# Maxima of the scores by four heads instead of two, and new instruction orders, in the first two of four passes of a decoder kernel

## What is computed

```python
x = _layernorm(x + _L0_attn_ref(x, Wq, Wk, Wv))              # self attention, 16 heads of 16
x = _layernorm(x + _L0_xattn_ref(x, ctx, ctx, ...))          # cross attention over 77 keys
x = _layernorm(x + _L0_ffn_ref(x, w_gate, w_up, w_down))     # quantized gated MLP
x = _layernorm(x + _L1_attn_ref(x, ...))                     # self attention with rotary embedding
x = _layernorm(x + _L1_xattn_ref(ctx, x))                    # alignment by dynamic time warping
x = _layernorm(x + _L1_ffn_ref(x, ...))                      # attention with gated heads
```

## Time and profile before

| | |
|---|---|
| median of 3 runs | 5856.48 us (5843.52 to 5859.08) |
| the profiled execution | 5858.39 us |
| its span in the profile | 5856.6 us |
| PE busy | 5289.1 us (90%) |
| DVE busy | 4889.5 us (83%) |
| ACT busy | 4166.3 us (71%) |
| POOL busy | 2753.9 us (47%) |

### The profile page before, as it was taken

How to read it: one execution, slowest core, us unless ns; L and a number is a source line. 1 busy time by engine, 2 the same in 40 slices (tenths; PEclk the granted TensorE clock), 3 DMA queues, 4 the chain that set the end, 5 groups by cost and what they waited for, 6 DMA issues and landing times. The chain is left out here.

```text
span 5856.6 us, 138862 instructions
## 1 busy us (share of the span) xinstructions
PE 5289.1 (90%) x54914; PEld 3660.6 (63%) x54914; DVE 4889.5 (83%) x11487; ACT 4166.3 (71%) x7921; POOL 2753.9 (47%) x2766
## 2 busy tenths in 40 slices
PE   6999999969999999987999999999308999999998
PEld 4666666646666666655666666666206667666666
DVE  6888888859999999986878778778677888888887
ACT  5777777748888888875666666666326777777776
POOL 0122111125555555543545545545106777777775
PEclk9999999989999999999999999999659999999999
DMA  1111111111111111001010010010110001101000
GB/s 55 45 45 45 48 45 46 45 36 30 30 30 30 31 30 29 30 23 35 30 34 30 30 34 30 30 34 30 38 30 14 31 26 31 31 26 31 28 29 23
DMA packets 140516, 194.01 MB, mean 33 GB/s; under 512 B 26080, under 2 KB 63840, under 8 KB 139488
## 3 DMA queue, kind: packets, MB, share of 16 engines
q1 hardware_dynamic: 139872, 185.13, 10.1%
HBM read 112.90 MB, written 72.18 MB: 32 GB/s over the span
## 5 line engine op out<-in xcount | busy, mean ns | idle before, releaser
L1020 ACT ACTIVATE Cpr<-pj 128x512 f32<-128x512 f32 x1024 | 522.2, 614 | 426.9 <-PE pj L814 426.9
L1206 DVE TENSOR_REDUCE Amp<-pj 128x2 f32<-128x512 f32 x1024 | 629.5, 682 | 97.8 <-PE pj L881 97.8
L1206 DVE TENSOR_REDUCE Cmp<-pj 128x2 f32<-128x512 f32 x1024 | 634.4, 682 | 77.7 <-PE pj L881 77.7
L1020 ACT ACTIVATE Apr<-pj 128x512 f32<-128x512 f32 x1024 | 522.1, 613 | 172.7 <-PE pj L814 172.7
L1206 DVE TENSOR_REDUCE Dmp<-pj 128x2 f32<-128x512 f32 x1024 | 633.2, 681 | 6.1 <-PE pj L881 6.1
L1020 ACT ACTIVATE Dpr<-pj 128x512 f32<-128x512 f32 x1024 | 520.2, 610 | 101.1 <-PE pj L814 101.0
L1134 POOL TENSOR_SCALAR Ave<-Amv 128x2 f32<-128x2 f32 x64 | 14.6, 228 | 971.7 <-DVE Amv L1274 971.7
L1106 POOL TENSOR_TENSOR Dnrm<-Dnrm,power 128x32 f32<-128x32 f32 x64 | 348.8, 5449 | 122.7 <-DVE Dnrm L1184 122.7
L700 POOL TENSOR_TENSOR Cqr<-Cqk,rope_cos 128x512 f32<-128x512 f32 x64 | 81.6, 1274 | 564.0 <-DVE Cqk L1174 564.0
L1141 POOL TENSOR_SCALAR Dx<-Dres,Dmv,Drstd 128x256 f32<-128x256 f32 x256 | 312.3, 1230 | 28.9 <-POOL Drstd L1135 28.9
L1141 POOL TENSOR_SCALAR Bx<-Bres,Bmv,Brstd 128x256 f32<-128x256 f32 x256 | 311.9, 1225 | 29.6 <-POOL Brstd L1135 29.6
(11 more groups left out here) (305 smaller groups left out, 15111.7 us busy)
## 6 DMA issues: line engine op xcount, KB each, us to landing
Ax0T<-in_xT SPq DMA_DIRECT2D x64, 256.0 KB, 3.0
Ax<-in_x SPq DMA_DIRECT2D x64, 256.0 KB, 3.0
x_A_scratch<-Ax SPq DMA_DIRECT2D x64, 256.0 KB, 2.1
Bx<-x_A_scratch SPq DMA_DIRECT2D x64, 256.0 KB, 2.9
x_B_scratch<-Bx SPq DMA_DIRECT2D x64, 256.0 KB, 2.0
Cx<-x_B_scratch SPq DMA_DIRECT2D x64, 256.0 KB, 3.1
x_C_scratch<-Cqr SPq DMA_DIRECT2D x64, 256.0 KB, 3.0
Dx<-x_C_scratch SPq DMA_DIRECT2D x64, 256.0 KB
```

The lines of the kernel that those rows point to most:

```text
L1020: ck.tell(act.activation(dst, ck.bank(step + (bank,))[0:n, :], ACT.Exp, scale=HD ** -0.5), "probs_ready", step)
L1206: ins = dve.tensor_reduce(dst, src, AX.X, ALU.max, negate=True)
```

## The change

`ROW_GROUPS` of A1 and A2 goes from 2 to 4. With it, A1 has four `max` steps of four heads in four banks where it had eight of two, and A2 has two steps of eight heads in four banks where it had four of two banks. The chain of A is four steps shorter, that of B two. The numbers of matmuls, of banks filled in a round and of reductions remain. As the steps are numbered anew, the orders of both phases are written anew for all five engines, and their steps are ordered otherwise than before. C, D and the path stage are not touched.

```diff
-ROW_GROUPS = {"A1": 2, "A2": 2, "A3": 4, "A4": 4}
+ROW_GROUPS = {"A1": 4, "A2": 4, "A3": 4, "A4": 4}
@@ ORDER, "A" @@
         "pe": (
-            505, 506, 617, 507, 618, 508, 620, 510, 723, 724, 402, 511, 512, 621, 403, 513, 514, 515, 301,
-            404, 516,
+            1306, 1308, 1309, 1417, 1310, 1311, 1202, 1419, 1312, 1203, 1204, 1313, 1101, 1205, 1420, 1314,
+            1316,
         "act": (
-            610, 502, 722, 613, 401, 617, 619, 620,
+            1013, 801, 1015, 1016, 908, 1018, 910, 802,
         "dve": (
-            723, 724, 511, 512, 403, 514, 515, 404, 516, 405, 406, 407, 408, 725,
+            1520, 1306, 1309, 1521, 1311, 1419, 1312, 1203, 1204, 1205,
         "pool": (
-            725,
+            1321,
         "sp": (
-            309, 526, 0,
+            522, 307, 0,
@@ ORDER, "B" @@
         "pe": (
-            106, 323, 217, 218, 324, 219, 325, 107, 220, 1, 108, 109, 110, 431, 2, 3, 111, 327, 432, 112, 4,
-            328, 113, 115, 5, 329,
+            207, 208, 530, 103, 209, 425, 210, 426, 104, 211, 213, 105, 427, 321, 215, 216, 106, 322, 217,
+            323, 218, 1, 2, 429,
         "act": (
-            531, 103, 426, 427, 212, 428, 104, 214, 216, 429, 323, 324, 219, 325, 430, 1, 108,
+            104, 212, 214, 321, 427, 322, 217, 323, 428, 1, 429, 107, 324, 3, 325, 326, 110,
         "dve": (
-            426, 102, 211, 322, 532, 427, 533, 428, 430, 105, 217, 218, 106, 324, 107, 325, 220, 221, 109, 110,
+            208, 530, 209, 320, 425, 426, 531, 428, 105, 215, 216, 106, 322, 323, 218, 219, 2, 324,
         "pool": (
-            833, 503, 521, 522,
+            303, 319, 320, 531,
         "sp": (
-            634, 100,
+            832, 300,
```

## The result

| | before | after |
|---|---|---|
| median | 5852.9 us (4 runs, 5843.5 to 5859.1) | 5890.8 us (4 runs, 5885.7 to 5894.8) |
| profiled execution | 5858.4 us | 5885.7 us |
| its span | 5856.6 us | 5883.9 us |

The changed kernel is slower: ratio 1.0065, 95% interval 1.0053 to 1.0078, or +38 us. The forecast was 5904 us, the range 5852 to 5948.

What follows compares the result with a forecast made beforehand. A was taken as bound by a closed loop of PE waits, B by DVE's queue and a competing path; profiled 5858.4 + 25 (A) + 22 (B) = 5905.4, median 1.9 lower, about 5904 us; range 5852 to 5948.

Steps and rivals of the forecast that it cites:

- A's closed loop of waits: Phase A: start-to-start hops between PE steps, waits included, sum to 18.44 us a round, 0.39 over before, +25 us.
- What is removed: PE time of maxima matmuls (L881) in A: 2.75 to 1.59 us a round, at most 1.16 less, 0.6 counted.
- The x0T wait: PE's wait in A (L772) for the transfer of x0T, 0.36 us a round, goes because the load is issued earlier.
- Places of the waits in A: PE idle before core0 (some 0.8 us a round), k and pv1 (0.4 to 0.5 and 0.3), max0 (0.2).
- The test that I set, and that failed: Phase A: the forecast is wrong if PE's idle time is under 1.6 us a round.
- B: Phase B: +0.34 us a round, +22 us; bounds -8 us if the path is covered, +45 if loads join it.
- the path from norm1 to DVE's down: Phase B: via oT, oproj, k, core0 and PE's down, 9.58 us against DVE's own 9.12, +0.46 a round.
- a link that was to disappear: Phase B: one exposed link in DVE's queue (gu, then hq) disappears, -0.12 us a round.
- The second test: Phase B: the forecast is wrong if DVE waits nowhere; a new wait at L1258 for PE's L951 was expected.
- rival 3: Phase B turns latency-bound as k's load lands late: 22.1 us a round, 5945 us; chance 0.12.
- C, D and the path stage: The parts outside phases A and B should be unchanged.

Runs made afterwards that it cites:

- short exponentials: Changed kernel with phase A's exponentials over 256 of a bank's 512 columns, half of A's probabilities left out: 5863.4 us, ratio 1.0010.
- four_f35: Kernel before with four heads a maxima step in A, another hand-made order of A, B as before: 5836.7 us, ratio 0.9968.
- after_pairs: Changed kernel with each maxima step of four heads sent as two pairs, same orders, banks and signals: 5896.5 us, ratio 1.0068.
- pairs_p12: Kernel before with two heads a maxima step kept, a new order of A, the load first on SP, B as before: 5767.6 us, ratio 0.9851.

## Why the prediction was right, point by point

**Sign and size** were right: +38 us between the medians, where the sum had +47. The 9 too many lie nearly all in B.

**A's closed loop of waits.** Forecast 18.44 us a round, measured 18.35; forecast +25 us, measured +23.6. Hop by hop, forecast and then as read above: shift0 to core0 1.09, 1.01; core0 to pv1 1.90, 1.81; pv1 to core1 1.86, 1.87; core1 to k 1.90, 1.81; k to max0 2.75, 2.73; max0 to v 0.36, 0.33; v to core2 1.83, 1.92; core2 to core3 5.67, 5.79; core3 to shift0 1.08, 1.08. The three hops with the large waits were taken 0.08, 0.09 and 0.09 too long, two hops of PE's own work 0.09 and 0.12 too short. The errors cancel in part, so the total is better than its parts, and that is luck. The short exponentials showed that two of these hops carry the round, and four_f35 that another order of the same steps takes 0.89 us less.

**What is removed.** L881 went to 1.59 us a round, as the earlier trace rows said, and of the 1.16 us less some 0.65 count from start to start, near my 0.6. The reason given was only half right. That a pair costs little in front of scores is true; that four row groups at once are what saves time is not, as after_pairs is as fast without them. By the span of the Trainium skill (TensorE: Matmul & The Clock Gate, "Measured speedup vs the span model") 1.37 was the estimate for halved packs; the trace says 1.59 with packs of four and 75.0 / 46.5 = 1.61 with twice as many packs of two, so the number of packs didn't set it here.

**The x0T wait** went, as forecast. It was priced at its idle time, 0.36 us a round, and is worth 0.56. The term was too small. It did no harm to the sum, which went by the loop and not by the difference to today's parts.

**Places of the waits in A.** Core0 and k are as forecast. Pv1 and max0 have next to none. In their place max2 stands 0.24 for exponentials: its banks are core3's last three and shift0's, which was on record with the orders and which the prediction did not price. That wait lies inside the hop from core0 to pv1 and costs nothing of its own: the hop takes the same 1.81 as core1 to k, where no such wait is, and with short exponentials the wait moves to pv1, where the prediction had it.

**The test that I set, and that failed.** I was to be wrong if PE's idle time in A were under 1.6 us a round. The groups give (26.8 + 21.0 + 11.9) / 46.5 = 1.28, and yet the loop holds. The 1.6 came from differences of starts, and idle time begins only at the end of the last matmul, when the next could have started already. By starts, the waits are 1.01 - 0.27 (core0), 1.39 - 1.08 (max2), 0.42 - 0.36 (pv1), 1.81 - 1.44 (k) and 2.73 - 2.56 (max0): 1.65 us a round, against the 2 of the forecast. With max2 and max3 at the 0.4 that the prediction took for them, and not at max0's 0.36, it is 1.57. So even by starts 1.6 was too near to what came to be a test.

**B.** Forecast +0.34 us a round and +22 us, measured +0.18 in the usual round and +14 us. The term that was mis-sized is the path from norm1 to DVE's down, forecast 0.46 longer than DVE's own work beside it; it is 0.12 longer. Both sides were off, the path 9.40 us where 9.58 was forecast and DVE's own work 9.28 where 9.12 was. The 0.12 us of a link that was to disappear are made up for by the seams at oproj and v. The second test held, barely: DVE waits at L1258 as foreseen, too briefly for the views to put a releaser to it. By the rule of the Trainium skill (TensorEngine Tiling (Array Packing), "PSUM Bottleneck") B was to stay as it is; a round 0.2 us longer is nearer to that than to my 0.34, and DVE, busy 1098.4 of 1160 us, is still its bound. Of rival 3, the late load came in single rounds, and not the 22.1 us a round.

**C, D and the path stage**: the two phases alone sum to the whole change, so next to nothing is left for them. From B's last v to the end of the span it is 5856.6 - 2561.6 = 3295.0 us before and 5883.9 - 2594.7 = 3289.2 after.

## What to carry to other kernels

In an order written by hand, what a step costs is not its length alone but what stands between it and the step that waits for it: follow the loop of such hops once round, start to start, and compare it with the work of each engine. Before a new order is judged, mend what else holds the old one up; here one load moved ahead of a store was worth 32 us, and the same wait, gone from the changed kernel, hid more than half of what the new order of A costs. A bigger pack is worth nothing where the small ones can stand side by side (75.0 against 74.1 us), and a small one in front of scores is partly covered by them; which size is better in itself these runs do not settle.

## What the runs showed of the hardware

Two packs of two row tiles, on different row groups and sent back to back, overlap as one pack of four: 75.0 and 74.1 us for 1488 matmuls of 32 rows by 256 columns in bf16.

A step on two row groups overlaps with a following fp32 score step on all four, which can start 0.01 us behind it; in pairs_p12 it then takes 0.13 to 0.23 us to that step's main part, instead of 0.31 in front of a transpose.

At the down step of B DVE starts a ready instruction 0.08 us before its predecessor's end (2017.31 against 2017.39), and one whose input comes just at that end 0.04 behind it (2002.61 against 2002.57). To be late by nothing at all costs 0.12 us there.
